# Convolution mixer: 64-column products, zero padding to 128, and the mix behind the taps

## What is computed

```python
inner = w_in.shape[1]                       # 192
h = _layernorm(x, n1_g, n1_b)
p = h @ w_in + b_in
local = conv3x3_depthwise(p, k_conv)        # SAME, one filter per channel
lr, rl = ema(local, axis=2), ema(local, axis=2, reverse=True)
tb, bt = ema(local, axis=1), ema(local, axis=1, reverse=True)
mixed = 0.25 * (lr + rl + tb + bt) + local
mixed = _layernorm(mixed, on_g, on_b)
x = x + (mixed @ w_out + b_out)
```

## Time and profile before

| what | value |
|---|---|
| median of three runs | 1242.63 us (1242.58 to 1251.63) |
| span of the profiled execution | 1243.8 us (the profile gives no other time for it) |
| PE busy | 1126.7 us, 91% of the span |
| DVE, ACT, POOL busy | 57%, 42%, 32% |
| mean granted TensorE clock | 0.957 of full |
| the mixer | from 217 us to 349 us of the span |

### The profile page before, as it was taken

How to read it: one execution, slowest core, us unless ns; L and a number is a source line. 1 busy time by engine, 2 the same in 40 slices (tenths; PEclk the granted TensorE clock), 3 DMA queues, 4 the chain that set the end, 5 groups by cost and what they waited for, 6 DMA issues and landing times. The chain is left out here.

```text
span 1243.8 us, 23469 instructions
## 1 busy us (share of the span) xinstructions
PE 1126.7 (91%) x8797; PEld 774.5 (62%) x8797; DVE 703.3 (57%) x2003; ACT 525.7 (42%) x855; POOL 395.0 (32%) x616
## 2 busy tenths in 40 slices
PE   5999988899989799999999986888898887999998
PEld 2677656577656566666666664665555544677776
DVE  3899633678724466666666664573556556323232
ACT  1666532466523343333333322444344322455453
POOL 4766463665363210101011204144001001254522
PEclk9999999799979899999999997787999998999999
DMA  6400000000000000000000000000000000000000
GB/s 123 83 2 2 2 1 0 1 2 1 1 1 0 1 1 1 1 2 1 1 1 1 1 1 1 1 1 1 1 2 1 2 1 1 1 13 7 14 7 14
DMA packets 28523, 9.32 MB, mean 7 GB/s; under 512 B 26689, under 2 KB 28416, under 8 KB 28416
## 3 DMA queue, kind: packets, MB, share of 16 engines
q1 hardware_dynamic: 25392, 6.95, 2.7%
q10 hardware_dynamic: 3024, 0.92, 0.4%
HBM read 6.29 MB, written 1.57 MB: 6 GB/s over the span
## 5 line engine op out<-in xcount | busy, mean ns | idle before, releaser
L156 POOL TENSOR_TENSOR ln_v<-MV,eps 128x2 f32<-128x2 f32 (+3 forms) x81 | 16.2, 200 | 421.4 <-PE bank L1133 243.5
L1195 ACT ACTIVATE fa_e<-bank 128x1024 f32<-128x1024 f32 x64 | 65.5, 1023 | 156.3 <-PE bank L1103 156.3
L1998 PEld LDWEIGHTS bank<-e_w,ex_G 128*128 128x128 f32 x768 | 90.6, 192 | 14.4 <-issue 14.4
L2113 DVE SCALAR_TENSOR_TENSOR X<-bank,ex_L,X 128x96 f32<-128x96 f32 x128 | 31.7, 310 | 114.6 <-PE bank L1998 108.8
L1247 DVE TENSOR_REDUCE fa_z<-bank 128x4 f32<-128x1024 f32 x64 | 77.9, 1217 | 25.3 <-PE bank L1085 23.3
L1990 PE MATMUL bank<-hT,e_w 96*128 96x512 f32 x192 | 91.4, 613 | 0.0
L2041 ACT ACTIVATE ex_G<-bank,e_b 128x512 f32<-128x512 f32 x96 | 64.4, 687 | 63.0 <-PE bank L1990 60.3
L1998 PE MATMUL bank<-e_w,ex_G 128*128 128x96 f32 x768 | 90.0, 274 | 0.0
L1845 DVE TENSOR_REDUCE ca_z<-bank 128x2 f32<-128x256 f32 x96 | 48.8, 551 | 48.9 <-PE bank L1572 48.8
L1103 PE MATMUL bank<-fa_a,fa_b 64*128 64x256 f32 x512 | 73.5, 406 | 1.1 <-DVE fa_a L1254 1.1
L159 POOL TENSOR_TENSOR ln_r<-ln_v,minus_half 128x2 f32<-128x2 f32 (+3 forms) x81 | 71.7, 886 | 0.0
(11 more groups left out here) (251 smaller groups left out, 2565.6 us busy)
## 6 DMA issues: line engine op xcount, KB each, us to landing
out_tokens<-X SPq DMA_DIRECT2D x8, 192.0 KB, 2.1
X<-in_x SPq DMA_DIRECT2D x14, 96.0 KB, 3.3
e_w<-in_L_ffn_w SPq DMA_DIRECT2D x2, 576.0 KB
bias0r<-in_L_conv_rpb_table ACTq DMA_DIRECT2D x16, 24.0 KB
m0w<-in_L_conv_mlp_w SPq DMA_DIRECT2D x2, 144.0 KB
m1w<-in_L_conv_w SPq DMA_DIRECT2D x2, 144.0 KB
f_w<-in_L_ffn_W SPq DMA_DIRECT2D x2, 142.5 KB
mixer<-in_mixer SPq DMA_DIRECT2D x1, 256.0 KB
```

The source lines that it names most:

```text
L1195: act.activation(E[v % 2][:], k.banks[:, b:b + 2, :].rearrange("p i (c q) -> p i c q", c=2), ACT.Exp).then_inc(s["exp"], 1)
L1998: last = pe.matmul(bank[4 + e % 2][:, t * C:(t + 1) * C], G[e % 2][:, j, t * P:(t + 1) * P], k.ew2[:, e, j, :], start=(j == 0), stop=(j == ...
```

## The change

A new helper `halves` issues a product as two, one for each half of the weight columns; `mix`, `out` and `widen` use it. `Z` is widened from 192 to 256 columns and the upper half of `ZT`'s second part is used, both filled with zeros once, by two memsets on POOL at the start of the phase; so the four transposes of `back` all have 128 columns and `out` always contracts over 128 rows. In PE's turn `mix(n-1)` moves from ahead of `back` to behind `taps`. The lists of DVE and ACT keep their order.

```diff
+def halves(pe, out, weights, moving, **flags):
+    for i in range(2):
+        columns = slice(64 * i, 64 * i + 64)
+        last = pe.matmul(out[columns], weights[:, columns], moving, **flags)
+    return last
...
-        Z = sb("z", [P, 2, CI])
+        Z = sb("z", [P, 2, 2 * P])
...
                 norm(0, 0)
+                pool.memset(Z[:, :, CI:2 * P], 0.0)
+                pool.memset(ZT[:, 1, :, :], 0.0)
                 for i in range(2):
                     last = pool.memset(grid[i][:], 0.0)
...  mix
-                            last = pe.matmul(mixed[n % 2][:, t * CI:(t + 1) * CI], k.mixer[:, j, t * P:(t + 1) * P], loc[:, j, :],
-                                             start=(j == 0), stop=(j == 1))
+                            last = halves(pe, mixed[n % 2][:, t * CI:(t + 1) * CI], k.mixer[:, j, t * P:(t + 1) * P], loc[:, j, :],
+                                          start=(j == 0), stop=(j == 1))
...  back
-                            last = pe.transpose(bank[5][0:part[j], (2 * j + t) * P:(2 * j + t + 1) * P], Z[:, t, j * P:j * P + part[j]], k.ident[:])
+                            last = pe.transpose(bank[5][:, (2 * j + t) * P:(2 * j + t + 1) * P], Z[:, t, j * P:(j + 1) * P], k.ident[:])
...  out
-                            last = pe.matmul(bank[6][:, t * C:(t + 1) * C], ZT[0:part[j], j, t, :], k.wout[0:part[j], j, :],
-                                             start=(j == 0), stop=(j == 1))
+                            last = halves(pe, bank[6][:, t * C:(t + 1) * C], ZT[:, j, t, :], k.wout[:, j, :],
+                                          start=(j == 0), stop=(j == 1))
...  widen
-                        last = pe.matmul(bank[1][:, j * TOK:(j + 1) * TOK], k.win[:, j * P:(j + 1) * P], k.hT[slot][:, 0:TOK], start=True, stop=True)
+                        last = halves(pe, bank[1][:, j * TOK:(j + 1) * TOK], k.win[:, j * P:(j + 1) * P], k.hT[slot][:, 0:TOK], start=True, stop=True)
...  the order of a turn
-                    if 1 <= n <= IMAGES:
-                        mix(n - 1)
                     if n >= 2:
                         back(n - 2)
                     if n < IMAGES:
                         taps(n, slot)
+                    if 1 <= n <= IMAGES:
+                        mix(n - 1)
                     if n + 1 < IMAGES:
                         widen(n + 1, 1 - slot)
```

More of the change, by code:

```diff
@@ L940, in normalised @@
                     for t in range(2):
-                        last = act.activation(Z[:, t, :], mixed[n % 2][:, t * CI:(t + 1) * CI], ACT.Identity, bias=o2[:, t, :], scale=r2[:, t, :])
+                        last = act.activation(Z[:, t, 0:CI], mixed[n % 2][:, t * CI:(t + 1) * CI], ACT.Identity, bias=o2[:, t, :], scale=r2[:, t, :])
                     last.then_inc(s["z2"], 1)
```

## The result

The changed kernel takes 1307.7 us (median of four runs, 1304.4 to 1309.3) where the kernel before took 1243.2: a ratio of 1.050 over all runs, 95% interval 1.047 to 1.053. The forecast was 1303 us, with a range of 1269 to 1323. The profiled execution has a span of 1307.5 us, 63.7 us more than before.

A forecast was written before the change was run, and what follows sets the result against it. PE's own list was taken to set the 7.12 us turn, with a 6.44 us loop just under it. Profiled span 1243.8, plus 57 for 14 turns at 11.2 us, plus 2.4 for edges, gave 1303 us, range 1269 to 1323.

The forecast's parts named there:

- The loop: Mixer turn: `cm_z`, `back` and `taps` join the chain through DVE, PE and ACT; 9.26 us at full clock against 7.12.
- The clock: PE's clock in the mixer: 60% of the 3.24 us a turn that half clock adds, making 11.2 us a turn.
- The first rival: Mixer: same loop, but PE stays at full clock; 1276 us, chance 0.25.
- The halves: 64-column halves in the mix run side by side: nothing gained or lost against the whole product, 1.50 us.
- The changes of shape: `widen` and `out`: any gain or loss lies off the loop, with 3.48 us available for the 2.4 us they took.
- the third rival: Mixer: PE is relieved and falls under DVE's 6.67 us turn; 6.7 us a turn, about 1238 us, chance 0.03.
- The edges: Memsets at the start, turn 1 and the mixer's end: together +2.4 us, between 0 and 5.

The follow-up runs named there:

- the waits filled: Changed kernel with unread bf16 products added in PE's two waits of a turn, ahead of `back`'s wait for `cm_z` and of `conv_t`'s for DVE: 1276.4 us.
- the old order: Changed kernel with mix(n-1) ahead of `back` and `taps` again, in two versions: mix in halves 1239.0 us, mix on the full array 1238.5 us.
- the mix first: Changed kernel with only the order undone: mix(n-1) ahead of `back` and `taps` again, in halves, padding kept: 1239.0 us, 0.996 of before.
- the seven other kernels: All follow-up kernels, each made by editing the changed kernel or the kernel before: medians from 1238.5 to 1310.9 us.
- `cm_z` ahead of `loc`: Changed kernel with ACT's normalised(n-1) moved to the end of turn n, ahead of loc(n): 1266.0 us, 1.018 of before.

## Why the prediction was right

Three rows of the middle turn before that are read below, of DVE, of `out`, and of the `conv_t` behind it:

```profile
290.22 0.25 DVE L987 BATCH_NORM_AGGREGATE cm_ag<-cm_st 128x2 f32<-128x6 f32 x2 [0.46 <-DVE cm_st L982]
...
291.88 1.53 PE L858 MATMUL bank<-w_out,cm_zT 128*128 128x96 f32 x8
...
293.34 0.33 PE L894 MATMUL bank<-ident,cm_acc 128*128 128x128 f32 x1
```

- *The loop.* Foretold 9.26 us at full clock, measured 9.25 with the waits filled. The check that made this possible was the last turn before the change, in which the old loop could be seen bare at 6.45 us; all that the change puts into it was then added from rows. In the filled kernel the mix follows the start of `taps` after 1.35 us (284.63 to 285.98), the value taken.
- *The clock.* The term known least, and a lucky one: 60% of the price of a turn at half clock was the middle of wide bounds, and the measured mean of 11.23 us falls on the forecast 11.2. That is (11.23 - 9.25) / 3.24 = 61% of the price. No single turn is like that: ten last 10.7 to 11.0 us and four 11.9 to 12.3. The first rival, in which the clock stays, was the filled kernel's 1276 us; its condition was not met.
- *The halves.* They run side by side in the mix: in the old place, both with a first load, 16 passes take 1.45 us until `back` (276.96 to 278.41) and eight whole ones 1.41 (287.53 to 288.94). The Trainium skill has a charge of about 60 cycles for each matmul (TensorEngine Tiling (Array Packing), Instruction Overhead). The prediction's estimate from it, some 5 us, counted eight products more of two passes each, where the mix has four more, eight passes; by the page that would be an estimate of 0.2 us a turn, some 3 us in all. It does not show: the eight passes more cost 0.04 us.
- *The changes of shape.* With 64 columns and 128 rows throughout, `out` takes 0.76 us until the next step (288.14 to 288.90) for 1.46 in the middle turn before (291.88 to 293.34). The padding and the halves came together here, and no run separates them. The Trainium skill's rule that a change of tiling mode drains TensorE (the same page, Key Properties) agrees with this; it was the rule for the third rival. With the old order that rival's time came true, 1239.0 and 1238.5 us against its 1238; the moved mix alone kept it from happening. Its reason did not quite: DVE was to set the turn with 6.67 us without a pause, but the first row above is a pause of 0.46 us in that stretch, and with the mix first DVE needs 6.51 us (269.03 to 275.54) and then waits for `cm_g`: the loop of two turns sets the turn.
- *The edges.* This is the term of the sum that was mis-sized: foretold +2.4 us, between 0 and 5 (its parts add up to 2.3), measured 63.7 - 57.6 = 6.1. The memsets at the start cost about the 0.4 us that was said: the phase starts 0.4 us earlier (PE's first transpose at 216.99 for 217.39 us), and the first `conv_t` comes at 228.19 in both. Turn 1 was to lose 1.4 us and gains 0.5 (7.29 for 7.77): the clock was at full 4.5 us earlier there, so `taps(1)` and the mix ran at 1.00. The end of the mixer, from the `conv_t` of turn 15 to DVE's last step, was to cost 0.5 and costs 1.1 (14.2 us for 13.1). The other 5.6 us lie behind the mixer, where both kernels run the same code: 900.5 us for 895.0, with 102 us at half clock for 86. In the seven other kernels that stretch took 892.1 to 895.6 us, with 76 to 90 at half clock. So I take the 5.6 us for stretches at half clock that fall otherwise when a stage starts at another time; no run tests it.

## What to carry to other kernels

A list in order that is 95% busy can have a loop through the other engines just under it, here 6.45 us under 7.12. Before a step is moved for the good of the busy engine, look for what that step feeds, write out that loop with what now stands ahead of the step, and look among the waits of the engines next door: here `back` needed a result that its engine makes right behind the one that the mix needs. Here waiting cost twice, as TensorE's clock fell with it; a kernel with the same loop and its waits filled with idle products shows how much is which. A loop can also be longer than one turn: with the mix first no engine is busy for more than 88% of the time, and a chain of two turns through DVE, PE and ACT sets the pace.

## What the runs showed of the hardware

*The clock fell with waits of one and two microseconds.* In the changed kernel PE waits 1.30 and 2.01 us in a turn of 10.93, and in the 14 turns the granted clock falls to 0.50 fourteen times. With `cm_z` ahead of `loc`, where of the two only the wait for DVE is left (29.1 us in 14 turns), it falls seven times. With the waits filled it stays at 1.00 for 129.79 us, and with the mix first, where PE waits 11.7 us in the 14 turns, for 95.81.

*DVE's first tap is held up by a step of POOL's.* The groups of instructions of DVE in the 14 turns, of the kernel before and then of the changed one (busy us, mean ns):

```profile
L1008 DVE TENSOR_SCALAR cm_acc<-cm_g,k_conv 128x256 f32<-128x256 f32 x14 | 5.0, 357 | 10.9 <-ACT cm_g L949 10.9
```

```profile
L1018 DVE TENSOR_SCALAR cm_acc<-cm_g,k_conv 128x256 f32<-128x256 f32 x14 | 7.6, 545 | 0.0
```

The instruction is the same. In the changed kernel it starts while POOL's step of the layer norm on the whole tile runs:

```profile
291.98 0.72 POOL L165 TENSOR_TENSOR Y<-X,MV 128x192 f32<-128x192 f32 x1
292.25 0.60 DVE L1018 TENSOR_SCALAR cm_acc<-cm_g,k_conv 128x256 f32<-128x256 f32 x1
```

The kernel with the mix first has both cases in one trace. In the turns at 269.03 and 282.77 (above) tap 0 starts as that step ends, and takes 0.35 us. In one turn it starts 0.36 us before the end:

```profile
289.28 0.72 POOL L165 TENSOR_TENSOR Y<-X,MV 128x192 f32<-128x192 f32 x1
...
289.64 0.51 DVE L1018 TENSOR_SCALAR cm_acc<-cm_g,k_conv 128x256 f32<-128x256 f32 x1
```

In both pairs of rows the tap ends 0.15 us behind POOL's step (292.85 for 292.70, 290.15 for 290.00), however early it began. The Trainium skill says that DVE and GpSimd share one pair of ports to the on-chip memory, and that a tensor_scalar can take it whole (SBUF — State Buffer, Who interferes with whom). The trace agrees with that in so far as the tap ends only behind POOL's step; no run moved one of the two alone. The three taps behind the residual are longer too with the mix first (1.77 us at 270.43, 1.50 at 287.65 in the middle turn before); their cause is not shown.
